# Second expert layer of a graph network on one core: run one tile ahead, with the operands turned by VectorE instead of TensorE

## The reference

```python
h = jnp.maximum(_layernorm(x), 0.0)
gates = softmax(h @ gate_W + gate_b); top_v, top_i = top_k(gates, 2)
def sage_conv(h, W_l, b_l, W_r):
    aggr = segment_sum(h[src], dst, num_segments=n) * inv_deg     # mean over the neighbours
    return aggr @ W_l + b_l + h @ W_r                             # means and own rows
for e in range(4):
    t = h
    for l in range(2):
        t = relu(sage_conv(t, Wl[e, l], bl[e, l], Wr[e, l]))
    expert_outs.append(t)
x = x + sum over the two chosen experts of gate * expert output
```

## Time and profile before

| | |
|---|---|
| median of 3 runs | 767.87 us (767.61 to 768.0) |
| the profiled execution's own time | 767.32 us |
| its span | 765.6 us |
| TensorE (PE) busy | 738.3 us, 96% of the span |
| VectorE / ScalarE / GpSimd busy | 394.7 / 288.2 / 120.6 us |
| mean granted TensorE clock | 0.995 of full speed |
| one tile of the second expert layer | 11.75 us |

### The profile page before, as it was taken

The page is one execution under the profiler, slowest core; times in us unless marked ns, Lnnn a source line. Parts: engine busy times, 40 slices in busy tenths (PEclk is TensorE's granted clock), DMA queues, the critical chain, the costliest instruction groups (busy, mean ns, idle before and its releaser), DMA issues.

```text
span 765.6 us, 11869 instructions
## 1 busy us (share of the span) xinstructions
PE 738.3 (96%) x3746; PEld 598.8 (78%) x3746; DVE 394.7 (52%) x982; ACT 288.2 (38%) x582; POOL 120.6 (16%) x134
## 2 busy tenths in 40 slices
PE   5899999999999999999999999899999999999994
PEld 3589977888888887777777777788888888888882
DVE  8898989988841558425426324432332333323320
ACT  6966678776552514214214213211121122112211
POOL 4000000000000104810000100232232332322211
PEclk9999999999999999999999999999999999999997
DMA  9000001111410456897896973498437943449900
GB/s 216 22 4 3 3 3 35 35 33 52 151 55 2 143 181 213 245 329 289 282 351 224 335 255 110 143 285 309 90 72 229 334 123 78 90 100 268 301 12 7
DMA packets 45321, 115.12 MB, mean 150 GB/s; under 512 B 7300, under 2 KB 7432, under 8 KB 45241
## 3 DMA queue, kind: packets, MB, share of 16 engines
q1 hardware_dynamic: 28581, 77.60, 30.9%
q0 software_dynamic: 8016, 19.59, 11.1%
q10 hardware_dynamic: 8644, 16.86, 7.0%
HBM read 64.85 MB, written 50.07 MB: 150 GB/s over the span
## 4 chain that ended last, share of the span: by engine, by line
PE 92%; DVE 4%; ACT 2%; issue 1%; POOL 0%; DVEq 0%; ACTq 0%; POOLq 0%
PE ps L1679 16%; PE ps L1680 15%; PE ps L1681 15%; PE ps L2090 7%; PE ps L2089 6%; PE ps L1948 3%; PE ps L1949 3%; PE ps L1881 3%; PE ps L1756 3%; PE ps L1875 3%; PE ps L1876 3%; PE ps L2011 2%; PE ps L2100 1%; PE ps L2055 1%; PE ps L1819 1%; PE ps L1707 1%
## 5 line engine op out<-in xcount | busy, mean ns | idle before, releaser
L2090 PE MATMUL ps<-slots,CTs 125*128 x230 | 91.0, 395 | 0.0
L2089 PE MATMUL ps<-slots,CTs 125*128 x207 | 81.7, 395 | 0.0
L996 ACT ACTIVATE slots<-he_t 125x512 fp32r<-125x512 f32 x40 | 25.4, 635 | 148.5 <-DVE he_t L1510 133.6
L1510 DVE TENSOR_TENSOR he_t<-ps,b_b 125x512 f32<-125x512 f32 x40 | 27.6, 691 | 102.8 <-PE ps L1681 71.0
L1603 DVE CAST CTs<-ps 125x512 fp32r<-125x512 f16 (+1 forms) x69 | 37.3, 596 | 76.4 <-PE ps L2011 76.4
L685 POOL DMA_INDIRECT out<-tg,rec x23 | 37.1, 1613 | 180.1 <-ACT tg L1046 164.3
L1679 PE MATMUL ps<-W,agT_hi 128*125 128x512 f32 x160 | 63.5, 397 | 0.0
L1679 PE MATMUL ps<-W,h2T_hi 128*125 128x512 f32 x160 | 63.4, 396 | 0.0
L1681 PE MATMUL ps<-W,agT_lo 128*125 128x512 f32 x160 | 63.3, 396 | 0.0
L1680 PE MATMUL ps<-W,agT_hi 128*125 128x512 f32 x160 | 63.2, 395 | 0.0
L1680 PE MATMUL ps<-W,h2T_hi 128*125 128x512 f32 x160 | 63.2, 395 | 0.0
(11 more groups left out here) (302 smaller groups left out, 1670.9 us busy)
## 6 DMA issues: line engine op xcount, KB each, us to landing
he_d<-slots SPq DMA_DIRECT2D x30, 448.0 KB
slots<-he_d SPq DMA_DIRECT2D x30, 448.0 KB
w_d<-slots SPq DMA_DIRECT2D x3, 4096.0 KB, 19.7
slots<-w_d SPq DMA_DIRECT2D x24, 512.0 KB, 20.8
t_d<-he_t SPq DMA_DIRECT2D x40, 224.0 KB
raw<-in_L_gnn_Wl ACTq DMA_DIRECT2D x4, 1024.0 KB, 8.9
raw<-in_L_gnn_Wr ACTq DMA_DIRECT2D x4, 1024.0 KB, 5.7
slots<-in_L_gnn_Wl ACTq DMA_DIRECT2D x4, 1024.0 KB, 9.4
```

The costliest lines, as they stand in the source:

```text
L996: a.activation(HE[:, t, 0:D], he_t[:, (x * T + t) % 4, :], ACT.Relu).then_inc(he_hi_ready.sem, 1)
L1510: v.tensor_tensor(he_t[:, n % 4, :], ps[0:P, bank_of(x, g, t), :], b1_b[:, x % 2, :], ALU.add).then_inc(pre_ready.sem, 1)
L2089: mm(o, CTs[:, t, :], part(k, P, t * 1024, P), start=False, stop=False)
L2090: last = mm(o, CTs[:, t, :], part(k, P, t * 1024 + D, P), start=False, stop=t == T - 1)
```

## The change

Four things change together.

1. **One tile ahead.** TensorE computes `neighbours(i + 1)` before `transformed(i)`, into two banks by turns. `turn_rows(i + 2)` stands between them. On ACT `mean(i + 1)` stands after `mean_high(i)`, and on DVE `counts_in(i + 2)` after `mean_low(i)`.
2. **Own rows turned by VectorE.** The 512 features of the first layer are written in another order (groups of 32 columns are permuted when the weights and the bias are copied), so that a quarter of a row in DRAM, 512 bytes, holds 32 features of each of the four blocks of 128. From tile 1 on `gather_hidden` makes four indirect DMAs, one for each quarter, which put every 32x32 block on the partitions where its transpose has to stand; then one VectorE `transpose` turns the 16 blocks of a tile. `hrow` has three buffers.
3. **Means turned by VectorE.** For tiles 1 to 21 ACT writes `agn` to DRAM (`mean_d`, 256 KB), waits until this has landed, and issues four DMAs that read it back in pieces of 512 bytes into `agx` (`spread_mean`); VectorE turns it (`turn_mean`).
4. Tile 0 and the last tile keep TensorE transposes for the means, tile 0 also for its own rows. A short piece of GpSimd work makes the indices of the quarters.

```diff
@@ gpsimd
             def gather_hidden(i):
-                gather(hrow[i % 4][:], t_d.rearrange("e p t d -> (e p t) d"), i, 1, hrow_in[i % 4])
+                if i == 0:
+                    gather(by_row(hrow[0]), t_d.rearrange("e p t d -> (e p t) d"), i, 1, hrow_in[0])
+                    return
+                for q in range(RQ):
+                    g.indirect_dma_start(hrow[i % HB][:, q, :], None, t_d.rearrange("e p t (r f) -> (e p t r) f", r=RQ),
+                                         bass.IndirectOffsetOnAxis(ap=piece_i[:, q, i:i + 1], axis=0)
+                                         ).then_inc(hrow_in[i % HB].sem, 16)
...
+                if i + HB < NT:
+                    pool.wait_ge(*hrow_used(i + 1))
+                    gather_hidden(i + HB)
@@ scalar
             def mean(i):
                 act.wait_ge(*agg_done(i + 1))
-                a.activation(agn[:], ps[:, 4, :], ACT.Copy, scale=rec[:, i, 4:5]).then_inc(agn_ready.sem, 1)
+                o, m = agn[:], ps[:, 3 + i % 2, :]
+                if i in (0, NT - 1):
+                    o, m = quartered(o), in_quarters(m)
+                a.activation(o, m, ACT.Copy, scale=rec[:, i, 4:5]).then_inc(agn_ready.sem, 1)
+
+            def spread_mean(i):
+                act.wait_ge(*agn_ready(i + 1))
+                act.dma_start(mean_d, agn[:]).then_inc(mean_moved.sem, 16)
+                act.wait_ge(*mean_moved(MEAN_MOVES * (i - 1) + 16))
+                for r in range(RQ):
+                    act.dma_start(agx[32 * r:32 * r + 32], mean_d.rearrange("(q c) (r f) -> r c q f", q=RQ, r=RQ)[r]
+                                  ).then_inc(mean_moved.sem, 16)
...
+            for i in range(1, NT):
+                turned_high(i)
+                gated(i - 1)
+                mean_high(i)
+                if i + 1 < NT:
+                    mean(i + 1)
+                if i + 2 < NT:
+                    spread_mean(i + 1)
@@ vector
+            def turn_hidden(i):
+
+                dve.wait_ge(*hrow_in[i % HB](16 * RQ * (i // HB + 1) if i % HB else 16 + 16 * RQ * (i // HB)))
+                dve.wait_ge(*heT_lo_ready(i))
+                v.transpose(by_pair(hT_f[:]), hrow[i % HB][:].rearrange("p q (k a) -> p q k a", k=KC)).then_inc(hrow_used.sem, 1)
...
+            def turn_mean(i):
+                dve.wait_ge(*mean_moved(MEAN_MOVES * i))
+                dve.wait_ge(*aggT_lo_ready(i))
+                v.transpose(by_pair(aT_f[:]), agx[:].rearrange("p q (k a) -> p q k a", k=KC)).then_inc(mean_turned.sem, 1)
...
+            for i in range(1, NT):
+                biased(i - 1)
+                turned_low(i)
+                if i + 1 < NT:
+                    counts_low(i + 1)
+                    turn_mean(i)
+                mean_low(i)
+                if i + 2 < NT:
+                    counts_in(i + 2)
+                if i + 1 < NT:
+                    turn_hidden(i + 1)
@@ tensor
+            k, he_here, w2_here = slot_of(0)
+            neighbours(0, k, he_here)
+            turn_rows(1)
             for i in range(NT):
-                k, he_here, w2_here = slot_of(i)
-                if i > 0:
-                    turn_hidden(i)
-                neighbours(i, k, he_here)
+                here = k, w2_here
                 if i + 1 < NT:
-                    turn_rows(i + 1)
+                    k, he_here, w2_here = slot_of(i + 1)
+                    neighbours(i + 1, k, he_here)
                 if i == 0:
-                    turn_means(i)
-                transformed(i, k, w2_here)
+                    turn_hidden()
+                if i + 2 < NT:
+                    turn_rows(i + 2)
+                transformed(i, *here)
```

More of the change, by code:

```diff
@@ L283, in gnn_kernel @@
         assert o6[0] <= 40960
[L286 to L290 removed]
+        piece_f = at("piece_f", [128, RQ, NT], F32, lg_at)
+        piece_i = at("piece_i", [128, RQ, NT], I32, lg_at + 384)
+        row_f = at("row_f", [S, NT], F32, mv_at)
+        assert 4 * RQ * NT <= 384 and lg_at + 768 <= lg_end and 4 * NT <= 96
+        crow = [at(f"crow_{k}", [S, N], F16, R4 + 32 + 2528 * k) for k in range(3)]
+        crow_lo = at("crow_lo", [S, N], F16, row_at - 512)
+        CTs = at("CTs", [P, T, S], F32R, 155648)
+        HB = 3
+        hrow = [at(f"hrow_{k}", [128, RQ, KC * 32], F32, 160768 + 2048 * k) for k in range(HB)]
+        hT_f = at("hT_f", [128, D], F32, 160768 + 2048 * HB)
+        agx = at("agx", [128, RQ, KC * 32], F32, 160768 + 2048 * (HB + 1))
+        aT_f = at("aT_f", [128, D], F32, row_at + 2048)
+        assert 160768 + (HB + 2) * 2048 <= R4 + 32 and R4 + 32 + 3 * 2528 <= 179168
         b2_b = at("b2_b", [S, NE, D], F32, 147456)
@@ L557, in _ @@
             for s in hrow_in:
[L558 removed]
+                sp.wait_ge(*s(16 if s is hrow_in[0] else 16 * RQ))
             load_expert(1)
@@ L667, in _ @@
             pool.wait_ge(*rec_in(16))
+            link(g.tensor_copy(row_f[:], i32(rec[:, :, 1])))
+            pool.dma_start(piece_d, row_f[:]).then_inc(default_out.sem, 16)
+            pool.wait_ge(*default_out(32))
+            for r in range(RQ):
+                pool.dma_start(piece_f[32 * r:32 * r + 32], piece_d.rearrange("(q c) i -> c q i", q=RQ)
+                               ).then_inc(rec_in.sem, 16)
+            pool.wait_ge(*rec_in(16 * (RQ + 1)))
+            for r in range(RQ):
+                link(g.tensor_scalar(piece_i[32 * r:32 * r + 32], piece_f[32 * r:32 * r + 32], float(RQ), float(r),
+                                     ALU.mult, ALU.add))
             def gather(to, rows, i, field, landed):
@@ L690, in _ @@
             pool.wait_ge(*w_lo_ready(KC * (cut_number(NE - 1, 1) + 1)))
-            for i in range(2):
+            for i in range(3):
                 gather_counts(i)
@@ L697, in _ @@
             pool.wait_ge(*pre_ready(NE * T))
-            gather_counts(2)
-            for i in range(2, 4):
-                gather_hidden(i)
+            gather_hidden(2)
             pool.wait_ge(*x2_out(32))
@@ L984, in cut_high @@
                     if k < 2:
-                        last = copy(W1[k][:, c, 0:D], raw[:, c, :])
+                        last = copy(in_quarters(W1[k][:, c, 0:D]), quartered(raw[:, c, :]))
                     else:
@@ L1538, in places @@
                 link(v.tensor_tensor(n_e[:], place[:, T - 1, :], total[:, T - 1, :], ALU.add))
-                link(v.tensor_scalar(nt_e[:], n_e[:], 0.0, None, ALU.is_gt))
+                link(v.memset(nt_e[:], 1.0))
                 for k in range(1, T):
@@ L1653, in _ @@
                 dve.wait_ge(*s(32 * NE * T // 4))
[L1654 to L1659, removed]
-                turned_low(i)
[L1661 to L1666, removed]
+            counts_low(0)
+            counts_in(1)
+            counts_low(1)
+            mean_low(0)
+            order_hidden()
+            turned_low(0)
+            counts_in(2)
+            turn_hidden(1)
+            for i in range(1, NT):
+                biased(i - 1)
+                turned_low(i)
+                if i + 1 < NT:
[6 more added lines that the diff above has]
+                    turn_hidden(i + 1)
             biased(NT - 1)
```

105 lines of the change are left out of this document (64 added, 41 removed).

## The result

The changed kernel took 814.76 us (median of 4 runs, 811.63 to 817.25), the kernel before it 767.93 us beside it on the same chip (767.61 to 769.52). The ratio is 1.060 (95% interval 1.057 to 1.064): slower by 6%. The profiled execution took 817.25 us, with a span of 815.4. The prediction had said 779, with 796 as the upper end.

The account below looks back on a forecast made before the run. TensorE, busy 96% of the span, was taken as the bound: 767.3 less 18.7 (18.6 transposes + 2.0 start - 1.9 end) gives 748.6, plus 30.6 of stalls beside three loads gives 779.2, said as 779; range 750 to 796.

Parts of the forecast that it names:

- loss beside the three loads: Tiles under expert loads: TensorE waits for the means, 10.2 us a load, 30.6 for three.
- What leaves TensorE: Every tile: own-row and means transposes go, 0.43 us a group, 18.6 us in all; a tile falls from 11.75 to 10.88.
- The operation that no trace showed: VectorE's turn of the means: 0.7 us taken, between 0.6 and 1.4.
- The length of a stalled tile: Tile waiting for means: period P = x + 5.0, x the read's landing offset, once that is over 10.88.
- Between loads: Means' path in quiet tiles: write 3.6, read 4.7, serial path 10.6 us under 10.88; no stall, little to spare.
- rival (d): Quiet tiles: write + read over 8.6 between loads too, 0.5 us in some 14 more tiles, 786; chance 0.1.
- Beside a load: Means' path under a load: write 5.1, read 9.8 by packet turns, serial path 17.2; two tiles lose 3.9 and 6.3 us.
- The clock: After stalls of 4 to 6 us the clock can fall; costs 0 to 2 us behind a load's last stall.
- GpSimd: POOL's work in each tile: 8.2 us, 9.2 with the start delay, of 10.88, so at no cost.
- rival (c): POOL becomes the bound: quarter gathers of 1.6 us make a tile need 11.8, total 767.5; chance 0.05.
- Rival (a): Beside loads: the means' path stays within the slack, faster at 749, range 747 to 756; chance 0.2.
- Rival (b): Beside loads: counts land at 13 us and become the bound, period 12.7 in 3.5 tiles a load, 767.5; chance 0.07.

Follow-up runs that it names:

- experiment 5: Kernel of experiment 1 with GpSimd's quarter gathers of tile 2 held until ScalarE has written the high part of tile 0's own rows: 768.27 us, ratio 1.0003.
- experiment 1: Changed kernel with every tile's means turned by TensorE, nothing through memory; one tile ahead and own rows by VectorE stay: 768.07 us, ratio 0.9998.
- experiment 7: Kernel of experiment 1 with GpSimd's order spread, at most six indirect DMAs without a wait: 756.76 us, ratio 0.983 to the kernel before.
- experiment 9: Kernel of experiment 1 with the second expert's load held until tile 1 is done, so the gather run has no load beside it: 767.88 us, ratio 0.9995.
- experiment 4: Changed kernel with the means read back as whole 2 KB rows, 128 pieces instead of 512 of 512 bytes: 803.32 us, ratio 1.0458.

## Why the prediction was wrong

The direction and its reason were right: slower, by TensorE waiting for VectorE's low part of the means beside each load. The size was not. On the profiled execution 779.2 corresponds to a span of 777.5 (the span is 1.7 us shorter than the time); it was 815.4. The 37.9 us between them:

| | predicted | measured | difference |
|---|---|---|---|
| loss beside the three loads | 30.6 | 16.3 + 26.8 + 19.3 = 62.4 | +31.8 |
| tile 1 held up (tile 2 at 509.1; at 499.5 in experiment 5) | 0 | 9.6 | +9.6 |
| 20 tiles at 10.80, not 10.88 | | | -1.6 |
| start, end and rounding, what is left | | | -1.9 |

The losses are the lengths over 10.8 us of the long tiles and of one neighbour at each load that is 0.2 to 0.5 over.

- **What leaves TensorE** was right: 10.80 us a tile against 10.88 (11.25 with the means on TensorE, experiments 1 and 7).
- **The operation that no trace showed**, the turn by VectorE, took 0.71 us where 0.7 was chosen.
- **The length of a stalled tile**, P = x + 5.0 with the read landed x after the tile's start, was right but for the clock. In the four long tiles x is 19.4, 17.1, 16.4 and 23.1, and they last 2.5, 2.1, 2.3 and 1.7 us longer than the formula gives.
- **Between loads** was nearly right: a write of about 4.2 and a read of about 5.0 for 3.6 and 4.7. Together they are over the 8.6 us of rival (d), and from the tile at 536.0 to that at 590.2 the turn slid from 4.1 to 5.5 us after the tile's start. But the slack took it up until the next load came: one tile took 11.3 us, the others 10.8 to 11.1, and TensorE waited for the means only in the four long ones. So (d) met its condition and cost next to nothing.
- **Beside a load** is the step that failed, by its terms. The write was put at 5.1 us (8 turns of 0.19 on top of 3.6) and took 9.3, 8.4 and 9.8, the first of them 5.3 before its first packet, then 4. The read was put at 9.8 (32 turns of 0.22, and 2.7 for the rest) and took 13.1 to 16.8, the longest of them 36 turns of 0.33, 12.0 us, behind some 5 without its packets. So the turns were too short (GpSimd's queue, which the forecast counted only in its upper bound, took 21% of the engines in the same stretch), and the time before the first packet was missed, 1.2 us between loads and 3 to 5.3 beside one. A write and a read pay it once each, one after the other. In the earlier trace rows it can't be told apart: the prediction read the 6.2 us between these landings as turns alone. What makes the delay (the load's issues standing ahead or the busy engines) is not settled. The forecast had two long tiles a load; there were one, two and one, since with such latencies a load, some 40 us long, is over after the first or second.
- **The clock** was put at 0 to 2 us, with slack to absorb it. The slower matmuls are the last twelve of the tile, behind the stall and on the path; they took 5.3, 4.9, 5.0 and 4.5 us instead of 2.8. Over the four long tiles that is 8.5 us of the 31.8.
- **GpSimd** was checked for its sum, 9.2 us of a tile (right, 0.95 a gather; rival (c) is out), and for nothing else. At the start there is no tile to pace it, and it issues 14 indirect DMAs without a break. This is the other step that failed: the prediction has no term for it, and it cost 9.6 us. That ScalarE and VectorE start late then is shown by experiments 1, 5, 7 and 9, and experiment 9 excludes the load. Why they do is open. GpSimd isn't the one held up: its gathers keep to 0.95 us. And no record of instruction code landing (queues q8 and q14) falls at the end of a late start in experiment 9: they are at 488.8 and 509.1. A run of gathers of another size or length, set at a quiet place, would narrow it; it wasn't tried, nor was the path through memory with no load at all.
- **Rival (a)**, hidden anyway, is out by the landings. **Rival (b)**, counts as the bound, was real and small: 1.3 us of waits in experiment 1, 0.9 the longest. In the changed kernel TensorE waited 3.3 us for them once, in the long tile from 736.4 us, where the means came later still.

Packets of DMA in the kernel after, 485.3 to 497 us, when only GpSimd's gathers ran:

```profile
DMA packets 305, 0.74 MB, mean 63 GB/s; under 512 B 128, under 2 KB 128, under 8 KB 304
...
q0 software_dynamic: 304, 0.72, 23.3%
```

On this queue 176 packets of over 2 KB carried the 0.72 MB, 4,096 bytes each, although all gathers but the first fetched pieces of 512: eight pieces share a packet. On ScalarE's queue 512 such pieces were 512 packets (experiment 4). The Trainium skill, "DMA: Bandwidth & Descriptors", section "SWDGE vs HWDGE vs iDMA", gives for a packet "≤4096 B preferably, ≤64 descriptors" where it describes GpSimd's path. The trace agrees there and disagrees for the hardware queue, as the prediction had taken it. The section's other rule, that an engine goes round its queues and changes at packet boundaries, agrees in the main with experiment 4: 576 packets in 12.0 us, 192 in 5.1.

The gain that the change was after is half there. Turning the own rows by VectorE, one tile ahead and with GpSimd's order spread, gives 1.7% (experiment 7). What it saves beside the kernel before is 22 x 0.43 = 9.5 us of transposes and the idle time of tile 0. Turning the means saves 21 x 0.43 = 9.0 us and comes out 46.7 to 50.7 us behind.

## What to carry to other kernels

A round trip through memory on the critical path is to be priced beside the heaviest load, as the sum of two latencies, and each has a part before its first packet that no bandwidth figure holds; the trace of a lone transfer doesn't show it. An engine's queue needs a look at its order as well as at its sum, above all in a prologue where nothing paces it. When two edits come in one change, undo them one at a time even if one of them explains the sign: the half that was worth having was hidden here by a fault of 11 us at another place.

## What the runs showed of the hardware that was not expected

- During an unbroken run of 14 or 15 indirect DMAs on GpSimd (17 to 19 us, one every 1.26 us) instructions of ScalarE and VectorE started 4 to 12 us after their inputs and their engine were ready, the last of them 1 to 3 us after the run's end. This was so with a load beside it and without (DMA share 0.28). In experiment 7, where no run is longer than 6, nothing of the kind is seen. Runs of 12 at about 690 and 710 us in the kernel after went with VectorE's casts 0.8 to 2.1 us late.
- With a load's issues standing in SyncE's queue, a 256 KB write on ScalarE's queue had its first packet some 5 us after its issue (1.2 between loads), and landed after 8.4 to 9.8 us (about 4.2 between loads).
- Waits of 9 to 12 us on TensorE were followed by matmuls 0.43 us apart, after the longest for all twelve that were left in the tile (granted clock 0.50, 1.2 GHz), so a stall behind which a dependent group of twelve stands cost 1.7 to 2.5 us more than its own length.
